# The stationary marks of a graph kernel, with four visits interleaved

## The reference, cut to what matters

```
xn = layernorm(x)
def gnn_layer(x, W, b):            # used twice
    h = x @ W.T + b
    agg = segment_sum(h[src], dst, num_segments=1250)
    return relu(agg)
q, k, v = xn @ Wq.T, xn @ Wk.T, xn @ Wv.T
q = softmax(q, -1) * dim ** -0.5;  k = softmax(k, -2)
attn = q @ (k.T @ v)
x = x + gnn(xn) + ((attn + xn) @ W1.T @ W2.T + attn + xn)
x = x + experts(layernorm(x))      # Sinkhorn gates, top 156 tokens for each of 8 experts
```

## Time and profile before

| | us |
|---|---|
| three runs | 468.04, 469.66, 470.31 |
| median | 469.66 |
| the profiled execution | 469.05 |
| its span | 467.3 |
| lying around the span | 1.75 |

### The profile page before, as it was taken

One profiled execution on the slowest core, in us unless ns is written; L12 is line 12 of the kernel. 1 busy time (PEld: TensorE's weight loads), 2 busy tenths in 40 slices (PEclk: granted clock), 3 DMA queues, 4 the chain that ended last, 5 costly groups with the idle time before them and its releaser, 6 DMA issues.

```text
span 467.3 us, 6438 instructions
## 1 busy us (share of the span) xinstructions
PE 449.9 (96%) x2449; PEld 349.5 (75%) x2449; DVE 312.4 (67%) x681; ACT 150.6 (32%) x274; POOL 64.0 (14%) x108
## 2 busy tenths in 40 slices
PE   8999999999999999999999999999999999778995
PEld 4788778777777777777779999777777776454783
DVE  5995799899987888887741110444546567777972
ACT  4686454332322323242222111222141116441110
POOL 3188210000000000000004000004100000005642
PEclk9999999999999999999999999999999989999998
DMA  7902002912000000002100000004744459106791
GB/s 214 283 9 90 1 0 63 239 16 93 14 1 0 2 0 1 1 1 85 41 1 2 1 1 3 0 0 126 241 135 130 140 163 391 62 1 229 255 350 71
DMA packets 20824, 40.42 MB, mean 87 GB/s; under 512 B 2936, under 2 KB 3266, under 8 KB 20787
## 3 DMA queue, kind: packets, MB, share of 16 engines
q1 hardware_dynamic: 18547, 32.55, 22.4%
q0 software_dynamic: 2240, 7.39, 4.3%
HBM read 30.10 MB, written 10.30 MB: 86 GB/s over the span
## 4 chain that ended last, share of the span: by engine, by line
PE 85%; DVE 8%; ACT 3%; DMA 1%; issue 1%; SPq 1%; POOLq 0%; DVEq 0%; ACTq 0%
PE ps L732 47%; PE ps L1022 9%; PE ps L954 9%; PE ps L845 5%; PE ps L717 3%; PE ps L1039 2%; ACT scrap_a L1397 2%; PE ps L1148 2%; DMA RAW_K<-in_WkT 1%; PE ps L1118 1%; PE ps L877 1%; PE ps L981 1%; PE ps L766 1%; PE ps L1061 1%; PE ps L1003 1%
## 5 line engine op out<-in xcount | busy, mean ns | idle before, releaser
L1685 DVE TENSOR_TENSOR RING_S<-every_home,HOME 125x512 bf16<-125x512 f16 x64 | 43.8, 684 | 0.0
L954 PE MATMUL ps<-AT,H1H 125*128 125x416 f32 (+1 forms) x108 | 38.0, 352 | 0.0
L954 PE MATMUL ps<-AT,H1L 125*128 125x416 f32 (+1 forms) x108 | 38.0, 351 | 0.0
L1683 DVE TENSOR_TENSOR RING_D<-places,PLACES 125x440 bf16<-125x440 f16 (+3 forms) x64 | 36.4, 569 | 0.0
L1022 PE MATMUL ps<-H2H,AT 125*125 125x512 f32 x90 | 36.1, 402 | 0.0
L1022 PE MATMUL ps<-H2L,AT 125*125 125x512 f32 x90 | 35.5, 394 | 0.0
L1039 PE MATMUL ps<-WE0H 128*128 128x512 f32 x125 | 35.4, 419 | 0.0
L1753 DVE TENSOR_TENSOR ps<-ps,bias 125x512 f32<-125x512 f32 x20 | 14.0, 700 | 28.7 <-PE ps L732 28.7
L1834 DVE SCALAR_TENSOR_TENSOR ZL<-ps,ZH 128x416 fp32r<-128x416 f32 (+1 forms) x12 | 6.3, 584 | 38.7 <-ACT ZH L1350 38.7
L606 POOL TENSOR_TENSOR G2L<-RAW_G,G2H 128x512 fp32r<-128x512 f32 x4 | 5.0, 1299 | 188.4 <-ACT G2H L1167 188.4
L1039 PEld LDWEIGHTS ps<-WE0H 128*128 128x128 f32 x125 | 22.8, 197 | 3.7
(11 more groups left out here) (401 smaller groups left out, 1175.6 us busy)
## 6 DMA issues: line engine op xcount, KB each, us to landing
RAW_E<-in_experts SPq DMA_DIRECT2D x8, 1024.0 KB, 9.2
RAW_AGAIN<-in_experts SPq DMA_DIRECT2D x3, 1024.0 KB, 8.8
X<-in_x SPq DMA_DIRECT2D x1, 2240.0 KB
out_x<-X SPq DMA_DIRECT2D x10, 224.0 KB
scratch<-X SPq DMA_DIRECT2D x10, 224.0 KB
scratch<-Y SPq DMA_DIRECT2D x10, 224.0 KB
RAW_K<-in_WkT SPq DMA_DIRECT2D x4, 256.0 KB, 5.1
RAW<-in_mW2T SPq DMA_DIRECT2D x1, 1024.0 KB, 12.8
```

What stands on the lines that cost most here:

```text
L954: pe.matmul(place(f), h[0:TT, k, 128 * f:128 * (f + 1)], AT[0:TT, k, c0:c1], start=(k == 0 and n == 0), stop=False)
L1683: V.tensor_tensor(hot_d(k, w), places[0:ET, 0:w].unsqueeze(1).broadcast_to([ET, BATCH, w]), PLACES[0:ET, c].unsqueeze(2).broadcast_to([ET, ...
L1685: V.tensor_tensor(hot_s(k), every_home[0:ET].unsqueeze(1).broadcast_to([ET, BATCH, 128]), HOME[0:ET, c].unsqueeze(2).broadcast_to([ET, BAT ...
```

## The change

The stationary marks of a batch were four arrays of 128 one behind the other. Now they are one array of 128 x 4 with the visit innermost: column 0 of visits 0 to 3, then column 1 of visits 0 to 3, and so on. `every_home` becomes a full array of 128 x 4, each number four times, where it was 128 numbers that line 1685 repeated by its access pattern. It takes 1024 bytes of a partition instead of 256, so all that is allocated behind it in area "a" lies 768 bytes further. The line for `HOME` now repeats its four numbers 128 times over (the innermost step is one element), where before each of the four numbers was repeated 128 times in a row (the innermost step was zero). PE reads the stationary operand of a visit with a step of four elements, 8 bytes. The moving marks stay as they were, in layout and in the instruction that makes them. Line 1802 belongs to a branch that runs only when an edge was left over by the visits.

No instruction is added, removed or moved on any engine; the order of all of them is the same.

```diff
-        every_home = small("every_home", [128, 128], F16, "a")
+        every_home = small("every_home", [128, 128, BATCH], F16, "a")
...
-        MARK_S = small("MARK_S", [128, RING_A, BATCH, 128], BF16, "a")
+        MARK_S = small("MARK_S", [128, RING_A, 128, BATCH], BF16, "a")
...
-        RING_S = at("RING_S", [128, RING_B, BATCH, 128], BF16, 125)
+        RING_S = at("RING_S", [128, RING_B, 128, BATCH], BF16, 125)
...
-            link(nc.gpsimd.iota(every_home[:], [[1, 128]], base=0, channel_multiplier=0,
+            link(nc.gpsimd.iota(every_home[:], [[1, 128], [0, BATCH]], base=0, channel_multiplier=0,
...
-                    mm = pe.matmul(PS[4 + g % 2][:, o:o + width(b)], hot_s(k)[:, v % BATCH, :], hot_d(k, width(b))[:, v % BATCH, :],
+                    mm = pe.matmul(PS[4 + g % 2][:, o:o + width(b)], hot_s(k)[:, :, v % BATCH], hot_d(k, width(b))[:, v % BATCH, :],
...
-                    V.tensor_tensor(hot_s(k), every_home[0:ET].unsqueeze(1).broadcast_to([ET, BATCH, 128]), HOME[0:ET, c].unsqueeze(2).broadcast_to([ET, BATCH, 128]),
+                    V.tensor_tensor(hot_s(k), every_home[0:ET], HOME[0:ET, c].unsqueeze(1).broadcast_to([ET, 128, BATCH]),
                                     ALU.is_equal).then_inc(done["marked"], 1)
...
-                        V.tensor_scalar(HOT_S[0:ET, a, :], every_home[0:ET, :], home[:, bass.ds(col, 1)], None, ALU.is_equal).then_inc(again[a], 1)
+                        V.tensor_scalar(HOT_S[0:ET, a, :], every_home[0:ET, :, 0], home[:, bass.ds(col, 1)], None, ALU.is_equal).then_inc(again[a], 1)
```

## The result

The changed kernel is a little slower. Its median is 470.64 us against 468.25 us for the kernel before, 22 runs of each; the ratio is 1.005, with a 95% interval from 1.0036 to 1.0064, which is a loss of 1.7 to 3.0 us. The forecast was 470.4 us, 0.75 us over before.

What follows compares the result with a forecast made beforehand. PE, without a gap, was taken to bound the marks' stretch. Terms of 0 (DVE), 0.75 (first loads), 0 (other loads) and 0 (POOL) on the median of 469.66 gave 470.4 us, range 468.0 to 473.0.

Steps and rivals of the forecast that it cites:

- PE bounds the stretch, DVE's gain is worth zero: In the 150 us where marks are made, PE has no gap; 21.4 us less of DVE gains nothing.
- Line 1685 at 420 ns, DVE's busy time near 106 us: Stationary marks on DVE: 81 instructions fall from 684 to 420 ns, busy time in the stretch from 127.3 to 106 us.
- The row of RS[1]: Line 1984 on DVE, 512 bfloat16 elements in the marks' new layout, 420 ns; taken as the forecast for line 1685.
- The new waits: Expected sign on DVE: longer waits for PE at lines 1691, 1753 and, newly, at 1683 for `visited`.
- The 16 weight loads held by marks cost nothing: Visit loads held by DVE, 4.5 us in all, delay no matmul; the rival that they did: 465.9 us, chance 0.05.
- The loads of the second to fourth visit are covered: Within a batch on PE, these 18 ns longer loads fit behind the matmul ahead and cost 0.
- The rival in which every load is seen: Each of the 322 visits on PE pays 18 ns, 5.8 us in all, 475.5 us; chance 0.11.
- The first load costs 0 to 18 ns a batch, middle taken, 0.75 us: On PE, each batch's first visit load isn't covered; over 81 batches 0 to 1.5 us.
- a sign of being wrong: The forecast is wrong if the visits' pieces of PE's chain grow by more than 0.02 us.
- POOL's longer iota costs zero, as the one that waits for it comes 17 us later: Line 638 on POOL writes 512 elements in about 1.7 us, ending near 61.5 us; its waiter starts at 79.1.
- The rule by which this term would be 0: SBUF line rule makes the 8-byte step of the visits' loads free: first-load term 0, forecast 469.7 us instead of 470.4.
- what I had called no change: Whole-kernel time within 0.5%, 2.3 us, of before: 467.3 to 472.0 us, chance 0.78.

Runs made afterwards that it cites:

- pairs_home_first: Changed kernel with visits interleaved in pairs (4-byte load step) and the 256-element every_home iota ahead of the twelve short ones; 468.22 us, ratio 0.9991 to before.
- strided_small: Changed kernel with the old 128-element every_home, repeated four times by access pattern; marks still interleaved; 469.39 us, ratio 1.0019 to before.
- home_first: Changed kernel with its long every_home iota moved ahead of the twelve short iotas on POOL; 469.46 us, ratio 1.0006 to before.
- pairs: Changed kernel with visits interleaved in pairs: 4-byte load step, every_home iota of 256 elements; 470.23 us, ratio 1.0041 to before.

## Why the prediction was right, point by point

- *PE bounds the stretch, DVE's gain is worth zero.* Right, and shown twice: on interleaved loads the marks that take 689 ns have the same stretch as those that take 418 (147.32), and pairs_home_first has the time of before with 21 us less of DVE.
- *Line 1685 at 420 ns, DVE's busy time near 106 us.* 418 ns and 105.58 us. The row of RS[1] was the right one. The new waits, though, came at lines 1706 and 1691, and at line 1753 (5.6 to 6.8 us); there is none at line 1683 for `visited`.
- *The 16 weight loads held by marks cost nothing.* Right: with fast marks they are 12, 3.4 us in all, and strided_small shows that faster or slower marks change no distance of PE.
- *The loads of the second to fourth visit are covered.* Right, 48.6 to 48.8 ns. The rival in which every load is seen, and the page "TensorE: Matmul & The Clock Gate" of the Trainium skill ("The mechanism"), by which a load overlaps a matmul only in another group of rows, would have made that 66; neither happened. What I had counted for that rival was a slip: at 0.5 ns a column, 110 columns are 55 ns and 80 are 40, so the visits' distances left nothing over, and not 8 ns.
- *The first load costs 0 to 18 ns a batch, middle taken, 0.75 us.* The mechanism was right and the size at the upper end: 17.4 ns, in 70 batches and not in 81, since ten stand behind transposes and one behind the small sums of line 870. 1.22 us. The nearest row had been there, 113 to 118 ns against 98, and nothing excused half of it. The chain's pieces of the visits grew by just under the 0.02 us that I had named as a sign of being wrong.
- *POOL's longer iota costs zero, as the one that waits for it comes 17 us later.* This is the step that failed. I asked who waits for POOL's result, and not what runs on DVE at the same time. In my own rows the iota stood at 59.8 us, and line 1558, a link of the chain, at 60.07. It cost 0.82 us on line 1558: home_first, which has the same iota at another time, gets them back, and pairs, with an iota of 1.51 us, loses 1.13 there. The estimate of 1.7 us for it was too long, too; it took 1.20.
- *The rule by which this term would be 0.* The page "SBUF — State Buffer" of the Trainium skill ("Door 1: The DMA port swizzle") has it that a step is free while two accesses fall in a line of 16 bytes. The runs disagree for weight loads with a step of 8 bytes, where 16 ns are seen in the record and 17 on the path; a step of 4 bytes was nearly free (98 ns, and 0.07 us in the stretch).

That the forecast of 470.4 us hit the level is luck: before's first three runs had stood 1.4 us above the median of the 22. On those 22 the loss is 2.4 us against my 0.75. Of the 1.65 us that were missing in my sum, 0.5 are the first loads, 0.8 the iota, and 0.3 aren't placed, well inside the interval. With that loss the time stands at the edge of what I had called no change.

## What to carry to other kernels

Ask of an engine's gain whether the engine that sets the pace ever waits for it; if it doesn't, the gain is worth nothing until something else is changed so that it would. Ask of a longer instruction on a side engine not only who waits for it, but also what runs beside it, and above all whether that is a link of the chain. And when the operands of small matmuls are laid out for the sake of the engine that writes them, read the step of the weight load off the trace at the place where a load isn't covered: the first one behind another kind of matmul.

## What the runs showed of the hardware

- An f32 TENSOR_SCALAR on DVE (80 x 250, 0.29 us) that began inside an iota on POOL ended 0.13 to 0.14 us behind it, with iotas of 0.37, 0.59, 1.20 and 1.51 us. TENSOR_TENSOR of 512 f32 elements beside it kept its 0.68 us, and SCALAR_TENSOR_TENSOR of 80 x 250 beside a short iota its 0.42 (before, 59.17 us).
- The time of a float16 iota depended on its pattern more than on its size: 512 elements took 0.59 us as four rows of 128 and 1.20 us with each number four times, while 256 with each number twice took 1.51.
- A bfloat16 weight load of 128 columns took 98 ns with a step of one or two elements and 114 with four.
- Going from f32 products to bfloat16 visits and back costs PE some 72 ns beyond four visits at 49 ns each, by the distances in the trace: 5 ns ahead, 5 on the first visit, 28 behind the last visit and 83 on the first product matmul, less one distance of 49. That was so 70 times in the kernel before. The 28 and the 83 also stand behind f32 transposes. Halving the places brought 1.3 us in the query stretch, a new wait of 0.8 us included.
